# Score matmuls of two quadrants issued together, with the half convolution tap behind them

## The chip, the cores and the metric

The kernel runs on one core of a Trainium2 chip. The metric is device time in microseconds (us) of one execution; three runs are shown for the kernel before. Engines: TensorE (PE, with its weight loads shown apart as PEld), VectorE (DVE), ScalarE (ACT), GpSimd (POOL), and SyncE (SP), which issues the loads and stores.

## The reference

The input is x of shape (32, 32, 16, 16) in fp32: 32 images of 32 channels and 16 x 16 = 256 pixels. Two blocks follow one another. The first is a bias-free layer norm, a channel attention with a depthwise convolution beside it, and an MLP whose hidden layer (128 channels) goes through a depthwise 3 x 3 convolution. The second is a pixel attention. What the change touches is the hidden convolution and the pixel attention:

```python
# MLP of the first block
h = _gelu(_conv(x, fc1_w, fc1_b))
h = h + _gelu(_conv(h, pos_w, pos_b, groups=h.shape[1], pad=1))
return _conv(h, fc2_w, fc2_b)
# second block, per image; q, k, v are (b, 256 pixels, 32)
scores = jnp.einsum('bic,bjc->bij', q, k)
a = jax.nn.softmax(scores, axis=1)
x = jnp.einsum('bij,bjc->bic', a, v)
return X + x
```

## The kernel before

**Layout.** Channels lie on the partitions, and 128 partitions hold four images: quadrant q is partitions 32q to 32q + 31. Eight slots of four images make the batch of 32; a chunk k is two slots, 2k and 2k + 1. The hidden layer has 128 channels, so one image fills all partitions there (`hpad`, padded to 18 rows of 17). PSUM (`ps`) has eight banks of 512 fp32 columns; `LOW` is banks 0 to 3, `HIGH` banks 4 to 7.

**Engines.** The order on every engine is written out by hand, and semaphores join them. TensorE's program is the list of calls from L488 on. The chunks take turns in the order 1, 2, 0, 3. While the pixel attention of one chunk runs, TensorE computes the hidden convolution of the next one.

**The convolution on TensorE.** `conv_taps(k, lo, hi, banks, groups, rows)` (L366 to L377) does taps of chunk k with diagonal 32 x 32 weights. One tap is 16 matmuls: for each bank g of four, one for each row quadrant r of the array, so that each of the array's 16 tiles of 32 x 32 is used once. The position of a tap in `TAP_ORDER` sets how many columns a matmul has: 512 for the centre, 480 for a shift in one direction, 450 for a corner. With `rows` cut to two quadrants a call does half a tap, 8 matmuls on half of the tiles. The last tap raises `conv_done`.

**The pixel scores.** `scores` (L451) computes the scores of a quadrant with matmuls of 32 rows and 128 columns of weights. `scores_beside_tap` (L460) does two quadrants of a slot with tiles of 32 x 32 instead, which leaves the other two row quadrants of the array free: each half `jt` of 128 pixels takes 2 x 4 = 8 matmuls of 256 columns. Between the two halves it issues half a tap of the next chunk's convolution on the two quadrants that the scores leave free (L470, L471). The last score matmul raises `scores_done`. The inner loops over q and c are one matmul each (L467).

There are four such calls, each after a wait for `exp_done`, ScalarE's count of finished exponentials, which says that the score banks are free again:

```python
scores_beside_tap(3, (0, 1), LOW, 5, HIGH)     # L586, waits exp_done 2
conv_taps(2, 6, 7, HIGH)
scores_beside_tap(3, (2, 3), LOW, 5, HIGH)     # L589, waits exp_done 4
conv_taps(2, 7, 9, HIGH)
values(1, 0)                                   # L592, waits exp_done 5
...
scores_beside_tap(5, (2, 3), HIGH, 6, LOW)     # L609, waits exp_done 10
conv_taps(3, 7, 8, LOW)
scores_beside_tap(5, (0, 1), HIGH, 6, LOW)     # L612, waits exp_done 12
fc2_units(0, 6)                                # L614, waits exp_done 13
```

Position 5 of the taps has 480 columns, position 6 has 450.

**Who reads the scores.** VectorE's `maxima` (L961 to L965) waits for `scores_done` and reduces each bank to its negated row maxima. ScalarE's `pixel_exp` (L742 to L753) waits for `max_ready` and turns a bank into exponentials, two instructions for each quadrant, with the row sums beside them, and raises `exp_done`.

**Around the calls.** `values` on TensorE (L441, matmuls at L448) projects the values of a chunk; VectorE's `values` (L955, L957) adds the bias into `v_tok`. After it VectorE does five `conv_steps` (L917; it does chunk 0's convolution itself) and `finish_block_slot` (L927), which writes `X` of chunk 2. TensorE waits for that `X` before `queries_and_keys` (L420). `fc2_units` (L413) is a product with weights of 128 rows.

Of the kernel before, what the change touches and what calls it, by code (L numbers as in the profile page):

```python
# [63 lines left out]
def quadrant(q):  # L64
    return slice(C * q, C * (q + 1))

def rotated(g, t):
    return (g + t) % G

def build(nc, x_in, first_in, second_in, third_in, out):
    with ExitStack() as ctx:
# [45 lines left out]
        def c3(name):  # L119
            return third[:, THIRD_COLS[name][0]:THIRD_COLS[name][1]]  # L120

        def slot(buf, s):
            return buf[:, s // 2, (s % 2) * NPIX:(s % 2 + 1) * NPIX]
# [7 lines left out]
        def padded(buf, first, n, tap):  # L131
            dy, dx = TAPS[tap]
            off = first * IMAGE + INNER + dy * ROW + dx
            return buf[:, off:off + n * IMAGE].rearrange("p (i y s) -> p i y s", i=n, s=ROW)[:, :, 0:SIDE, 0:SIDE]

        def inside(images, tap):
            dy, dx = TAPS[tap]
            return images[:, :, max(0, -dy):SIDE - max(0, dy), max(0, -dx):SIDE - max(0, dx)]

        def pixels(ap):  # L140
            return ap.rearrange("p (i y s) -> p i y s", y=SIDE, s=SIDE)

        def h_first(k, g):
            return (G * k + g) * 2
# [111 lines left out]
        def _(pe):  # L256
# [109 lines left out]
            def conv_taps(k, lo, hi, banks, groups=range(G), rows=range(G)):  # L366

                for i in range(lo, hi):
                    tap = TAP_ORDER[i]
                    for g in groups:  # L370
                        for r in rows:
                            last = pe.matmul(inside(pixels(ps[quadrant(rotated(r, g)), banks[g], :]), tap),  # L372
                                             c3("taps")[quadrant(r), tap * C:(tap + 1) * C],
                                             inside(padded(hpad[quadrant(r), :], h_first(k, g), 2, tap), tap),
                                             start=i == 0, stop=i == 8)
                if hi == 9:
                    last.then_inc(conv_done, 1)  # L377
# [82 lines left out]
            def scores_beside_tap(s, quadrants, banks, tap, conv_banks):  # L460

                rows = [r for r in range(G) if r not in quadrants]
                for jt in range(2):
                    for q in quadrants:
                        for c in range(G):
                            at = jt * P + c * C
                            last = pe.matmul(ps[quadrant(c), banks[q], jt * NPIX:(jt + 1) * NPIX],  # L467
                                             slot(swapped, s)[quadrant(q), at:at + C],
                                             slot(rstd, s)[quadrant(q), :], start=True, stop=True)
                    if jt == 0:  # L470
                        conv_taps(s // 2 + 1, tap, tap + 1, conv_banks, rows=rows)  # L471
                last.then_inc(scores_done, 1)

            def weighted_values(s, bank):

                if s < SLOTS - 1:
                    pe.wait_ge(v_scaled, slot_turn(s) + 1)
                for jt in range(2):
                    if s == SLOTS - 1:
                        pe.wait_ge(last_v_scaled, jt + 1)  # L480
                    for g in range(G):
                        at = jt * P + g * C
                        last = pe.matmul(ps[quadrant(g), bank, 0:NPIX], v_tok[:, s, at:at + C],  # L483
                                         prob[:, G * (slot_turn(s) % PROBS) + g, jt * NPIX:(jt + 1) * NPIX],
                                         start=jt == 0, stop=jt == 1)
                last.then_inc(av_done, 1)
# [97 lines left out]
            conv_taps(2, 3, 5, HIGH)  # L584
            pe.wait_ge(exp_done, 2)
            scores_beside_tap(3, (0, 1), LOW, 5, HIGH)  # L586
            conv_taps(2, 6, 7, HIGH)
            pe.wait_ge(exp_done, 4)
            scores_beside_tap(3, (2, 3), LOW, 5, HIGH)  # L589
            conv_taps(2, 7, 9, HIGH)  # L590
            pe.wait_ge(exp_done, 5)
# [15 lines left out]
            conv_taps(3, 4, 6, LOW)  # L607
            pe.wait_ge(exp_done, 10)
            scores_beside_tap(5, (2, 3), HIGH, 6, LOW)  # L609
            conv_taps(3, 7, 8, LOW)  # L610
            pe.wait_ge(exp_done, 12)
# [557 lines left out]
```

## Time and profile before

| what | us |
|---|---|
| runs | 119.53, 121.95, 118.51 |
| median of the runs | 119.53 |
| the profiled execution, its own time | 119.45 |
| its span, first to last instruction | 117.7 |
| TensorE matmul busy | 101.3 |
| TensorE weight loads busy | 58.4 |
| ScalarE busy | 86.7 |
| VectorE busy | 75.2 |
| GpSimd busy | 12.1 |

Busy times are unions over the span, so two matmuls on different tiles at the same moment count once, and a matmul's time runs from its start to the landing of its last column. A row of the timeline merges instructions of one kind that start near each other: its start, the time from the first start to the last end, and their count. What stands in square brackets at a row's end is how long the engine had been idle before it and what ended that. The chain of work that ended last is followed back from the end: each piece is what the next one had waited for, or what stood before it on its engine.

### The profile page before, as it was taken

Reading aid. Unit: us, or ns where it says so; the run is one execution under the profiler, and the core shown is the slowest. Engines: PE = TensorE matmul, PEld = TensorE weight load, DVE = VectorE, ACT = ScalarE, POOL = GpSimd, SP = SyncE. Lnnn points to the kernel's source line nnn. Section 1 sums busy time; section 2 is a strip of 40 time slices with the busy share of each in tenths; the row PEclk is TensorE's granted clock in tenths of the full one; section 3 lists DMA queues with packets and bytes.
Section 4 is the critical chain, followed back from the end, with each engine's and each line's share of the span. In section 5 each row is a group of like instructions: output and inputs, shape, how many; then the busy total and the mean of one; then the engine's idle time right before and its main releaser. Section 6 shows DMA issues by size and latency. Waiting matters only on the chain.

```text
span 117.7 us, 5736 instructions
## 1 busy us (share of the span) xinstructions
PE 101.3 (86%) x2632; PEld 58.4 (50%) x2632; DVE 75.2 (64%) x152; ACT 86.7 (74%) x204; POOL 12.1 (10%) x22
## 2 busy tenths in 40 slices
PE   0394999789999899998999799999799999997660
PEld 0042677566684446832445464534364566575330
DVE  0007992133332989799957698964746579789851
ACT  4069991851785883889567989947889989898960
POOL 5010000000000000000000000598000040002300
PEclk9999999995589999999999999999999999999999
DMA  2880000000000000000000000000000020002022
GB/s 61 277 336 16 0 6 6 0 6 0 6 6 6 8 0 6 8 6 0 6 0 6 0 6 6 0 0 6 6 6 0 0 95 0 6 15 77 0 89 89
DMA packets 1751, 3.42 MB, mean 29 GB/s; under 512 B 320, under 2 KB 576, under 8 KB 1728
## 3 DMA queue, kind: packets, MB, share of 16 engines
q1 hardware_dynamic: 1584, 3.03, 7.4%
q8 instruction: 20, 0.33, 1.2%
q10 hardware_dynamic: 144, 0.03, 0.2%
q14 instruction: 3, 0.02, 0.1%
HBM read 2.01 MB, written 1.05 MB: 26 GB/s over the span
## 4 chain that ended last, share of the span: by engine, by line
PE 64%; ACT 16%; DVE 11%; DMA 3%; issue 3%; ACTq 0%; DVEq 0%
PE ps L372 13%; PE ps L295 10%; ACT prob L749 6%; PE ps L455 6%; PE ps L420 4%; PE ps L483 4%; ACT hpad L700 4%; DVE unit L917 3%; DMA first<-first_in 3%; PE ps L284 3%; PE ps L262 3%; PE ps L467 3%; PE ps L448 3%; ACT prob L736 3%; PE ps L307 2%
## 5 line engine op out<-in xcount | busy, mean ns | idle before, releaser
L372 PE MATMUL ps<-hpad,third 32*32 32x450 f32 (+2 forms) x864 | 36.5, 563 | 0.6 <-ACT hpad L700 0.5
L749 ACT ACTIVATE prob<-ps,smax 128x256 f32<-128x256 f32 x56 | 25.7, 479 | 3.7 <-DVE smax L964 3.7
L917 DVE SCALAR_TENSOR_TENSOR unit<-hpad,third,unit 128x544 f32<-128x544 f32 x32 | 23.8, 796 | 0.0
L964 DVE TENSOR_REDUCE smax<-ps 128x2 f32<-128x512 f32 x26 | 16.5, 683 | 6.5 <-PE ps L467 3.4
L372 PEld LDWEIGHTS ps<-hpad,third 32*32 32x32 f32 x864 | 14.0, 103 | 8.9 <-issue 4.2
L295 PE MATMUL ps<-npad,second 32*32 32x225 f32 (+2 forms) x576 | 14.6, 390 | 0.3 <-DVE npad L841 0.3
L239 POOL TENSOR_TENSOR v_tok<-v_tok,row_inv 128x256 f32<-128x256 f32 x7 | 5.1, 738 | 94.0 <-DVE row_inv L974 94.0
L700 ACT ACTIVATE hpad<-ps,third 128x1024 f32<-128x1024 f32 x8 | 8.7, 1116 | 4.5 <-PE ps L356 2.4
L749 ACT ACTIVATION_READ_ACCUMULATOR prob<-ps,smax 128x1 f32 x56 | 11.8, 211 | 0.0
L295 PEld LDWEIGHTS ps<-npad,second 32*32 32x32 f32 x576 | 9.2, 107 | 3.4 <-issue 1.7
L483 PE MATMUL ps<-prob,v_tok 128*32 128x256 f32 x128 | 8.1, 382 | 2.3 <-ACT prob L736 1.1
L669 ACT ACTIVATE swapped<-ps 128x512 f32<-128x512 f32 x8 | 4.4, 593 | 7.1 <-PE ps L262 7.1
L841 DVE SCALAR_TENSOR_TENSOR npad<-x,first,rstd 128x256 f32<-128x256 f32 x8 | 3.5, 479 | 9.5 <-ACT rstd L678 9.5
L455 PE MATMUL ps<-rstd,swapped 32*128 32x256 f32 x96 | 8.4, 397 | 0.5 <-ACT swapped L718 0.5
L262 PE MATMUL ps<-x,first 32*32 32x256 f32 x64 | 3.9, 566 | 4.9 <-DMA first<-first_in 4.9
L455 PEld LDWEIGHTS ps<-rstd,swapped 32*128 32x128 f32 x96 | 5.9, 184 | 3.7 <-DVE rstd L934 2.1
L273 PE MATMUL ps<-swapped,first 32*32 32x256 f32 x128 | 6.0, 508 | 1.7 <-ACT swapped L669 1.7
L709 ACT ACTIVATE acc<-ps,third 128x512 f32<-128x512 f32 x12 | 7.3, 688 | 0.0
L483 PEld LDWEIGHTS ps<-prob,v_tok 128*32 128x32 f32 x128 | 4.0, 109 | 6.2 <-issue 2.8
L467 PE MATMUL ps<-rstd,swapped 32*32 32x256 f32 x128 | 5.8, 384 | 1.2 <-ACT prob L749 1.2
L675 ACT ACTIVATE rstd<-ps,eps_col 128x512 f32<-128x512 f32 x8 | 5.4, 679 | 1.8 <-PE ps L273 1.8
L420 PE MATMUL ps<-X,third 32*32 32x256 f32 x128 | 6.4, 382 | 0.2 <-DVE X L927 0.2
(83 smaller groups left out, 140.4 us busy)
## 6 DMA issues: line engine op xcount, KB each, us to landing
x<-x_in SPq DMA_DIRECT2D x4, 256.0 KB, 5.2
y<-m SPq DMA_DIRECT2D x3, 256.0 KB, 2.5
third<-third_in SPq DMA_DIRECT2D x1, 456.5 KB, 6.5
second<-second_in SPq DMA_DIRECT2D x1, 453.5 KB, 5.4
y<-m SPq DMA_DIRECT2D x2, 128.0 KB, 1.9
first<-first_in ACTq DMA_DIRECT2D x1, 33.0 KB, 4.1
```

Of the source, the lines that this page charges most:

```text
L262: last = pe.matmul(ps[quadrant(rotated(g, s)), banks[s % 4], 0:NPIX], c1("centre")[quadrant(g), :], slot((x, res1)[ln], s)[quadrant(g), :] ...
L295: last = pe.matmul(inside(pixels(ps[quadrant(rotated(g, s)), banks[t], 0:NPIX]), tap), c2("attn_taps")[quadrant(g), tap * C:(tap + 1) * C] ...
L372: last = pe.matmul(inside(pixels(ps[quadrant(rotated(r, g)), banks[g], :]), tap), c3("taps")[quadrant(r), tap * C:(tap + 1) * C], inside(p ...
L420: last = pe.matmul(ps[quadrant(rotated(g, s)), bank, half * NPIX:(half + 1) * NPIX], c3(w)[quadrant(g), :], slot(X, s)[quadrant(g), :], st ...
L455: last = pe.matmul(ps[:, banks[q], jt * NPIX:(jt + 1) * NPIX], slot(swapped, s)[quadrant(q), jt * P:(jt + 1) * P], slot(rstd, s)[quadrant( ...
L467: last = pe.matmul(ps[quadrant(c), banks[q], jt * NPIX:(jt + 1) * NPIX], slot(swapped, s)[quadrant(q), at:at + C], slot(rstd, s)[quadrant( ...
L483: last = pe.matmul(ps[quadrant(g), bank, 0:NPIX], v_tok[:, s, at:at + C], prob[:, G * (slot_turn(s) % PROBS) + g, jt * NPIX:(jt + 1) * NPI ...
L700: act.activation(padded(hpad, h_first(k, g), 4, CENTRE), two(banks).rearrange("p g (t y s) -> p (g t) y s", t=2, s=SIDE), ACT.Gelu, bias=c ...
L709: act.activation(acc_buf(k, g), ps[:, banks[g], :], ACT.Gelu, bias=c3("pos_b")[:, g:g + 1]).then_inc(conv_gelu, 1)
L749: last = act.activation(prob[:, G * (slot_turn(s) % PROBS) + g, jt * NPIX:(jt + 1) * NPIX], ps[:, banks[q], jt * NPIX:(jt + 1) * NPIX], AC ...
L917: dve.scalar_tensor_tensor(out=sums, in0=source, scalar=weight, in1=sums, op0=ALU.mult, op1=ALU.add).then_inc(unit_step, 1)
L964: dve.tensor_reduce(smax[:, s, 2 * q:2 * q + 2], ps[:, banks[q], :].rearrange("p (j i) -> p j i", j=2), AX_X, ALU.max, negate=True).then_i ...
```

## The change

`scores_beside_tap` issues the matmuls of both halves one after the other, 16 in all, then raises `scores_done` on the last of them, and only then issues the half tap. The same matmuls are issued on the same operands and banks. The four calls and everything around them stay as they are.

```diff
--- before.py
+++ after.py
@@ -467,9 +467,8 @@
                             last = pe.matmul(ps[quadrant(c), banks[q], jt * NPIX:(jt + 1) * NPIX],
                                              slot(swapped, s)[quadrant(q), at:at + C],
                                              slot(rstd, s)[quadrant(q), :], start=True, stop=True)
-                    if jt == 0:
-                        conv_taps(s // 2 + 1, tap, tap + 1, conv_banks, rows=rows)
                 last.then_inc(scores_done, 1)
+                conv_taps(s // 2 + 1, tap, tap + 1, conv_banks, rows=rows)
 
             def weighted_values(s, bank):
 
```

TensorE's program at the first two calls (L586, L589), as a difference of the two orders; L467 is a score matmul, L372 a matmul of a tap, and the number at a row's end is how many stand together:

```order
 L372 MATMUL ps<-hpad,third 32x2x15x15 x16
 L372 MATMUL ps<-hpad,third 32x32x15 x16
-L467 MATMUL ps<-rstd,swapped 32x256 x8
+L467 MATMUL ps<-rstd,swapped 32x256 x16
 L372 MATMUL ps<-hpad,third 32x32x15 x8
-L467 MATMUL ps<-rstd,swapped 32x256 x8
 L372 MATMUL ps<-hpad,third 32x2x15x15 x16
-L467 MATMUL ps<-rstd,swapped 32x256 x8
+L467 MATMUL ps<-rstd,swapped 32x256 x16
 L372 MATMUL ps<-hpad,third 32x32x15 x8
-L467 MATMUL ps<-rstd,swapped 32x256 x8
 L372 MATMUL ps<-hpad,third 32x2x240 x16
```

The eight scores of the second half have moved ahead of the half tap (the `x8` of L372), which now stands directly ahead of the full tap (`x16`).

TensorE's program at the last two calls (L609, L612), with the product over 128 rows (L413) behind the second of them:

```order
 L372 MATMUL ps<-hpad,third 32x32x15 x32
-L467 MATMUL ps<-rstd,swapped 32x256 x8
+L467 MATMUL ps<-rstd,swapped 32x256 x16
 L372 MATMUL ps<-hpad,third 32x2x15x15 x8
-L467 MATMUL ps<-rstd,swapped 32x256 x8
 L372 MATMUL ps<-hpad,third 32x2x240 x16
-L467 MATMUL ps<-rstd,swapped 32x256 x8
+L467 MATMUL ps<-rstd,swapped 32x256 x16
 L372 MATMUL ps<-hpad,third 32x2x15x15 x8
-L467 MATMUL ps<-rstd,swapped 32x256 x8
 L413 MATMUL ps<-unit,third 32x512 x4
```

Here it is the same move; in the last call the half tap now stands between the scores and L413.

## Rows read from the trace of the kernel before

**Rows 1.** The page: TensorE's busy time among the engines', and the chain by engine.

```profile
PE 101.3 (86%) x2632; PEld 58.4 (50%) x2632; DVE 75.2 (64%) x152; ACT 86.7 (74%) x204; POOL 12.1 (10%) x22
...
PE 64%; ACT 16%; DVE 11%; DMA 3%; issue 3%; ACTq 0%; DVEq 0%
```

**Rows 2.** The chain in order of time, first pair: start us, us, what.

```profile
69.40 1.96 PE ps L372 x58
71.36 1.10 PE ps L448 x8
...
72.49 0.69 DVE v_tok L957
...
73.29 2.40 DVE unit L917 x3
...
77.51 0.80 DVE X L927 x2
...
78.36 0.45 PE ps L420 x8
```

**Rows 3.** The same chain, from the second pair on.

```profile
84.81 0.45 PE ps L467 x8
...
88.30 1.00 PE ps L413 x8
...
104.31 1.09 PE ps L455 x8
...
105.42 0.70 DVE smax L964
```

**Rows 4.** The timeline of VectorE, first pair: start us, us, instruction, [idle before].

```profile
67.34 1.29 DVE L964 TENSOR_REDUCE smax<-ps 128x2 f32<-128x512 f32 x2 [0.93 <-PE ps L467]
...
72.49 0.69 DVE L957 TENSOR_TENSOR v_tok<-ps,third 128x512 f32<-128x512 f32 x1 [0.37 <-PE ps L448]
```

**Rows 5.** The timeline of ScalarE at slot 3's first quadrant.

```profile
68.06 0.47 ACT L749 ACTIVATE prob<-ps,smax 128x256 f32<-128x256 f32 x1 [0.36 <-DVE smax L964]
...
68.89 0.20 ACT L749 ACTIVATION_READ_ACCUMULATOR prob<-ps,smax 128x1 f32 x1
```

**Rows 6.** The timeline of TensorE, first call, and its wait for X.

```profile
65.94 0.45 PE L467 MATMUL ps<-rstd,swapped 32*32 32x256 f32 x8 [0.62 <-ACT prob L749]
66.00 0.64 PE L372 MATMUL ps<-hpad,third 32*32 32x480 f32 x8
66.18 0.59 PE L467 MATMUL ps<-rstd,swapped 32*32 32x256 f32 x9
66.43 0.61 PE L372 MATMUL ps<-hpad,third 32*32 32x480 f32 x8
66.59 0.50 PE L467 MATMUL ps<-rstd,swapped 32*32 32x256 f32 x8
66.83 0.54 PE L372 MATMUL ps<-hpad,third 32*32 32x450 f32 x1
66.83 0.47 PE L467 MATMUL ps<-rstd,swapped 32*32 32x256 f32 x7
67.04 1.22 PE L372 MATMUL ps<-hpad,third 32*32 32x450 f32 x31
...
78.36 0.45 PE L420 MATMUL ps<-X,third 32*32 32x256 f32 x8 [0.24 <-DVE X L927]
```

**Rows 7.** Line L467: its matmul passes, ns min/median/max.

```profile
L467 PE MATMUL ps<-rstd,swapped x128: 372/375/399, 65.9 to 87.9; 32*32 32x256 f32 x128
```

**Rows 8.** The timeline of TensorE, third call.

```profile
84.81 0.45 PE L467 MATMUL ps<-rstd,swapped 32*32 32x256 f32 x8 [0.59 <-ACT prob L749]
84.87 0.61 PE L372 MATMUL ps<-hpad,third 32*32 32x450 f32 x8
85.05 0.59 PE L467 MATMUL ps<-rstd,swapped 32*32 32x256 f32 x9
85.27 0.59 PE L372 MATMUL ps<-hpad,third 32*32 32x450 f32 x8
85.46 0.50 PE L467 MATMUL ps<-rstd,swapped 32*32 32x256 f32 x8
```

## Prediction

> **What bounds the kernel now.** I began with the page. TensorE (PE) is the busiest engine, 101.3 of 117.7 us, and the chain of work that ended last runs 64% through it, against 16% for ScalarE (ACT) and 11% for VectorE (DVE) [rows 1]. The share alone doesn't say that PE sets the time at the four calls that change, so I read the chain in order of time next. Around the first two calls it goes along PE without a break from 65.94 to 71.36 us, through the scores (L467), the convolution taps (L372) and into the value projection (L448); there it passes to DVE, which turns the projected values into v_tok at 72.49, does five steps of its own convolution and writes X, and at 78.36 PE takes up again on that X [rows 2]. From 84.81 on it is PE again, through the third and fourth calls and on to a score product that ends at 105.40; then the tail of maxima, exponentials and the last products ends the program [rows 3].
>
> So both pairs of calls lie on the path. The engines beside PE confirm it. DVE stands idle for 0.93 us before the maxima of 67.34 and for 0.37 us before v_tok at 72.49, both times until a matmul ends [rows 4]; ACT waits 0.36 us at 68.06 for the maximum [rows 5]. The value product at 71.29 waits for the fifth set of exponentials (exp_done 5). Slot 2 gives four of these, and the first quadrant of slot 3 has its two exponentials from 68.06 on, with the last read-out over at 69.09 [rows 5]: more than two us early. PE reaches the value product when its own queue is through, and no earlier exponential would bring it forward.
>
> The telling place is the second half's eight scores. Their tiles are free from 66.42 on (66.18 + 0.24). One of them begins there: the group of 66.18 counts nine instead of eight and ends 0.59 later, so its ninth pass began at 66.18 + 0.59 - 0.37 = 66.40. The others don't: the next group begins at 66.59 [rows 6]. In program order the call's matmuls are 1 to 8 (scores), 9 to 16 (tap), 17 to 24 (scores). Number 17 runs, number 18 comes 0.04 us after number 1 has ended (66.18 + 0.37 = 66.55). The same again behind the taps: of the next full tap one record starts at 66.83, the next ones at 67.04, when tap matmul number 9 has ended at 66.43 + 0.56 = 66.99. The reading that fits both: PE looks across about 17 matmuls from the oldest unfinished one, starts any whose tile is free, and takes in another only when the oldest has ended. The third call repeats it: 84.81, 84.87, 85.05, 85.27, and then 85.46 where the tiles were free at 85.29 [rows 8].
>
> The Trainium skill ("TensorE: Matmul & The Clock Gate", spec table and the step-by-step section of part 2) gives TensorE a queue of 64 with a partial reorder window that pulls weight loads ahead, while matmuls stay in program order. The depth agrees with this trace (16 matmuls with two loads and two passes each are 64 records). The strict order doesn't: the first scores' second passes start at 66.18, after passes of the tap that stands behind them. By strict order nothing would overlap in either version and the edit would be worth nothing.
>
> **The change, part by part.** Nothing is added or removed: in each of four calls the same 8 + 8 + 8 matmuls are issued as 8 + 8 + 8 with the tap last. No DMA, bank, semaphore or wait on another engine changes; `scores_done` hangs on the last score as before. The order pieces show what moves: 16 score matmuls stand together and the tap joins the full tap behind it.
>
> What it takes: the tap becomes numbers 17 to 24. Number 17 can start at once, 18 to 24 only when number 1 ends, at 66.59, in place of 66.00. Until then two row quadrants of the array stand still. What it gives: the second half's scores are in the window from the start, and go at 66.40 to 66.45 (eight starts 7 ns apart, as the first half's) instead of 66.59 to 66.69. Their last second pass begins 0.22 later, at 66.66 or so, and ends at 67.03 instead of 67.30, where the group of 66.83 ends [rows 6], so `scores_done` comes 0.27 us earlier in a call that starts from an idle PE (first and third). I cost that gain at nothing: what it feeds is DVE's 0.93 us idle and ACT's exponentials, and PE waits for neither, as shown above. It costs nothing the other way either.
>
> The price on PE: number 18 enters at 66.59 in both versions, and the matmul that can enter when 18 ends is ready accordingly. Before, 18 is a score and ends 0.61 later, at 67.20; after, it is a tap matmul and ends 0.99 later, at 67.58. The 35th matmul, and behind it the last six of the following tap, go 0.38 us later. I stepped both orders through with these four rules (tile free, 17 open, end in order, 17 ns between entries once the queue is full). For the order of before this gives 71.37 for the end of the last tap behind the second call and 88.30 for the last score of the fourth, where the chain has 71.36 and 88.30 [rows 2, 3]. For the changed order it gives:
> - first and second call, tap of 480 columns: 0.38 us each, 0.75 in all after rounding;
> - third call, tap of 450 columns: 0.40 to the second pass (84.87 to 85.27) and 0.54 for that pass, 0.94 against 0.61: 0.33 us [rows 8];
> - fourth call, the same tap, but behind it comes a product over 128 rows (L413), which starts when everything has drained [rows 3]. Before, the last to drain is a score at 88.30; after, it is the tap's last matmul, 0.27 us behind what the third call already moved.
>
> Sum: 0.75 + 0.33 + 0.27 = 1.35 us. The bounds of a call's price: nothing, if the quadrants really work apart; and the tap wholly exposed, 8 tap matmuls alone at 0.99 + 0.05 = 1.04 us less the 0.27 that the scores come earlier, 0.77. I take the stepped value because it reproduces two ends of before.
>
> Does it arrive at the end? The first 0.75 moves L448, then v_tok, which DVE awaits with 0.37 us of idle [rows 4]; DVE then has no gap up to X, and PE awaits X at 78.36 [rows 2]. If PE had slack there, the 0.75 would vanish; PE idles 0.24 us there until DVE has X [rows 6], so the late side is DVE's and nothing is absorbed. The other 0.60 stands at 88.30, and PE runs on from there to 105.40 without waiting [rows 3]. So 119.45 (the profiled execution's own time: 117.7 span and what lies around it) + 1.35 = 120.80 us. The median of the runs shown is 119.53, 0.08 above the profiled one, too little to correct for.
>
> **Rivals.**
> 1. *The quadrants hide it.* Per tile the work is unchanged: rows of the scores 4 x 0.22 to 0.24 = 0.9 us, rows of the tap 2 x 0.43 = 0.86. If the tap may start whenever its tiles are free, the call takes 0.9 in either order and the time stays at 119.5. For it: the tap does start 0.06 us after the scores in the present order. Against it: the score of 66.59 with its tile free at 66.42. The Trainium skill ("TensorEngine Tiling (Array Packing)", key properties) says that different tiles execute in parallel and independently; by that alone the sum is zero, and the pause at 66.42 speaks against taking it alone.
> 2. *Faster.* The maxima come earlier: 0.27 us in the first and third call. If the exponentials set when PE may go on, this comes through, 119.45 - 0.54 = 118.9 us. It decides from the point where PE waits for exp_done behind a call. For it: PE did wait for ACT 0.62 us at 65.94 [rows 6] and 0.59 at 84.81 [rows 8]. Against it: those waits are ahead of the calls, not behind them.
> 3. *The tap stands bare.* The window opens for the tap only as the last score ends, so each call costs 0.77: 4 x 0.77 = 3.1, 122.5 us. Place: behind the sixteenth score. Against it: number 18 starts in the trace while 9 to 17 are under way.
> 4. *Only the first pair counts.* Between 88.3 and 105.4 ACT and DVE wait too, and the chain may change hands there: 119.45 + 0.75 = 120.2 us.
>
> **How the numbers follow.** The forecast has 0.68, rival 1 0.12, rival 2 0.07, rival 3 0.07, rival 4 0.06. The likeliest is 120.8 us. The range goes from 119.4 (rival 1, below it only rival 2) to 122.0 (a price per call of 0.64, between stepped and bare). About 2%, 2.4 us, is what a measurement of this kernel can tell from no change. Slower by more needs 121.9 or above: rival 3 and a sliver of the forecast, 0.08. Faster by more needs under 117.1, which no case gives: 0.01. Within 2%: 0.91.
>
> **What would show it.** In the profile after: one group of 16 score passes from 65.94 with the second half's first pass at about 66.40; the tap's first passes at about 66.59 but for one; maxima at 67.07 in place of 67.34; L448 at about 72.0 in place of 71.29; v_tok 0.75 later; L413 some 1.35 later than 88.23. If L448 stands at 71.3 and the tap starts near 66.2, rival 1 holds. If DVE's or ACT's chain carries the earlier maxima to the end, rival 2. If the tap starts at 67.0, rival 3. The forecast is wrong altogether if PE's stretch from scores to L448 is as long as before.

## The result, and the profile after

The changed kernel's first four runs have a median of 121.25 us (120.72 to 124.97), the kernel before 119.07 (118.51 to 121.95, four runs). The ratio is 1.0222 with a 95% interval of 1.0157 to 1.0286. Measured again with twelve runs, it has a median of 121.09 us against 119.84 (35 runs of the kernel before). Both ratios compare only the undisturbed executions, since some executions of either kernel take some per cent longer than the rest; in the second comparison the ratio is 0.9995 (0.9930 to 1.0061). The two intervals don't meet, and neither holds the 1.011 that 1.35 us would be: the times scatter by more than the effect and settle neither its size nor, by themselves, its sign, so both have to be read in the traces.

The page and the chain of the changed kernel; below the busy time per engine, the chain in order of time: start us, us, what.

```profile
PE 101.2 (85%) x2632; PEld 57.0 (48%) x2632; DVE 75.5 (63%) x152; ACT 86.9 (73%) x204; POOL 12.1 (10%) x22
...
PE 64%; ACT 15%; DVE 11%; issue 4%; DMA 4%; ACTq 0%; DVEq 0%
```

```profile
73.17 0.69 DVE v_tok L956
...
79.04 0.45 PE ps L420 x8
...
89.58 1.00 PE ps L413 x8
...
106.70 0.70 DVE smax L963
```

TensorE's busy time over the whole span, 101.2 us against 101.3 [rows 1], doesn't show the loss, because ahead of the calls something else differs: the kernel before ran there for 6.8 us at the lower of the two clock levels (1.2 of 2.4 GHz, granted clock 0.50 from the 27th to the 33rd us) and was busy for 56.08 us up to the first call, the changed kernel had no such stretch and 54.68. From the first call to the maxima at 105.42 and 106.70 it is busy for 38.42 us before and 39.77 after, 1.35 more: the same passes side by side less often. The chain takes the same way [rows 2, 3], and each step is late. The first call starts at 65.87, 0.07 us earlier than before; X is taken up at 79.04 instead of 78.36, L413 stands in the chain at 89.58 instead of 88.30, the maximum behind the last chained score product at 106.70 instead of 105.42: 1.28 us later, and with the 0.07 of the start 1.35.

The timeline of TensorE in the changed kernel, first call, then the two products that follow the pairs, and the third call's start.

```profile
65.87 0.67 PE L467 MATMUL ps<-rstd,swapped 32*32 32x256 f32 x16 [0.63 <-ACT prob L748]
66.30 0.56 PE L372 MATMUL ps<-hpad,third 32*32 32x480 f32 x1
66.33 0.42 PE L467 MATMUL ps<-rstd,swapped 32*32 32x256 f32 x8
66.52 0.60 PE L372 MATMUL ps<-hpad,third 32*32 32x480 f32 x2
...
66.59 0.37 PE L467 MATMUL ps<-rstd,swapped 32*32 32x256 f32 x1
66.61 1.69 PE L372 MATMUL ps<-hpad,third 32*32 32x480 f32 x36
...
71.97 1.16 PE L448 MATMUL ps<-third,X 128*128 128x128 f32 x8
...
85.49 0.67 PE L467 MATMUL ps<-rstd,swapped 32*32 32x256 f32 x16 [0.60 <-ACT prob L748]
...
89.51 1.07 PE L413 MATMUL ps<-unit,third 128*32 128x512 f32 x8
```

Compare with [rows 6]. The sixteen passes of the first half run through (65.87), the second half's first passes follow at 66.33, without the pause before. The tap, which had begun 0.06 us behind the scores, now has one matmul at 66.30 and the rest from 66.52 on: 0.65 us behind the call's start, just when the first score has ended. From the first call to L448 it is 71.97 - 65.87 = 6.10 us (before 71.29 - 65.94 = 5.35), from the third call to L413 89.51 - 85.49 = 4.02 (before 88.23 - 84.81 = 3.42). Sum of the two losses: 0.75 + 0.60 = 1.35 us.

VectorE in the changed kernel, in order of time:

```profile
67.07 1.29 DVE L963 TENSOR_REDUCE smax<-ps 128x2 f32<-128x512 f32 x2 [0.73 <-PE ps L467]
...
73.17 0.69 DVE L956 TENSOR_TENSOR v_tok<-ps,third 128x512 f32<-128x512 f32 x1 [0.95 <-PE ps L448]
```

The maxima of the first call did come earlier (67.07 against 67.34 in [rows 4], 0.20 after taking off the earlier start), and it is worth nothing: before v_tok VectorE now waits 0.95 us for L448 where it waited 0.37.

### The profile page after: what moved, and what is told of

Its sections match the earlier page's. It is cut to its first block, busy times and chain, and to the rows that moved or that the text cites. A ratio compares the mean times of both kernels' runs of the same rounds, so it can differ in the third digit from the quotient of the medians.

```text
span 118.9 us, 5736 instructions
## 1 busy us (share of the span) xinstructions
PE 101.2 (85%) x2632; PEld 57.0 (48%) x2632; DVE 75.5 (63%) x152; ACT 86.9 (73%) x204; POOL 12.1 (10%) x22
## 2 busy tenths in 40 slices
DMA packets 1751, 3.42 MB, mean 29 GB/s; under 512 B 320, under 2 KB 576, under 8 KB 1728
## 4 chain that ended last, share of the span: by engine, by line
PE 64%; ACT 15%; DVE 11%; issue 4%; DMA 4%; ACTq 0%; DVEq 0%
PE ps L372 13%; PE ps L295 11%; ACT prob L748 6%; PE ps L455 6%; PE ps L420 4%; PE ps L482 4%; DMA first<-first_in 4%; DVE unit L916 3%; PE ps L284 3%; PE ps L356 3%; PE ps L448 3%; ACT prob L735 3%; PE ps L262 3%; PE ps L467 2%; PE ps L273 2%
## 5 line engine op out<-in xcount | busy, mean ns | idle before, releaser
L372 PE MATMUL ps<-hpad,third 32*32 32x450 f32 (+2 forms) x864 | 37.2, 563 | 0.6 <-issue 0.4
L372 PEld LDWEIGHTS ps<-hpad,third 32*32 32x32 f32 x864 | 14.5, 103 | 10.5 <-issue 5.6
L295 PE MATMUL ps<-npad,second 32*32 32x240 f32 (+2 forms) x576 | 14.3, 367 | 1.6 <-issue 1.3
L295 PEld LDWEIGHTS ps<-npad,second 32*32 32x32 f32 x576 | 7.9, 103 | 5.6 <-issue 4.1
L273 PE MATMUL ps<-swapped,first 32*32 32x256 f32 x128 | 5.3, 446 | 1.5 <-ACT swapped L668 1.4
L467 PE MATMUL ps<-rstd,swapped 32*32 32x256 f32 x128 | 5.3, 378 | 1.2 <-ACT prob L748 1.2
```

The costliest lines, as they stand in the source:

```text
L273: last = pe.matmul(ps[quadrant(g), banks[s % 4], 0:NPIX], c1("mean")[quadrant(q), :], slot(swapped, s)[quadrant(q), :], start=True, stop=True)
L295: last = pe.matmul(inside(pixels(ps[quadrant(rotated(g, s)), banks[t], 0:NPIX]), tap), c2("attn_taps")[quadrant(g), tap * C:(tap + 1) * C] ...
```

## The experiments

In all of them two distances are read in the profile: from the first call's start to L448, and from the third call's start to L413. Before they are 5.35 and 3.42 us, changed 6.10 and 4.02.

**The changed kernel again** (no edit).

> The changed kernel once more, unaltered, to settle its size. Theory (17 matmuls open in order, price on TensorE's path): +1.35 us in the profile between the start of the first call and the product L413, and about 1.1 to 1.2% in the time. The first ratio, 1.022, would be 1.2 us more than that path shows; if it comes again, half of the loss lies outside the two pairs of calls or in something the profile of one execution does not carry. Rival (tiles work apart): ratio 1.00.

```profile
65.74 0.66 PE L467 MATMUL ps<-rstd,swapped 32*32 32x256 f32 x16 [0.64 <-ACT prob L748]
...
71.84 1.16 PE L448 MATMUL ps<-third,X 128*128 128x128 f32 x8
...
85.36 0.67 PE L467 MATMUL ps<-rstd,swapped 32*32 32x256 f32 x16 [0.59 <-ACT prob L748]
...
89.38 1.07 PE L413 MATMUL ps<-unit,third 128*32 128x512 f32 x8
```

6.10 and 4.02 us again, to the hundredth. The times are those of the second comparison above: the first ratio's 2.2% doesn't come again, and the 1.1 to 1.2% that was expected isn't shown by it either. Of the scatter there is more at the end.

**One pair at a time.** Two kernels, against the kernel before. The first has the new order in the first pair of calls; in the second kernel 3 and 5 stand the other way round:

```diff
-                    if jt == 0:
+                    if jt == 0 and s == 5:
                         conv_taps(s // 2 + 1, tap, tap + 1, conv_banks, rows=rows)
                 last.then_inc(scores_done, 1)
+                if s == 3:
+                    conv_taps(s // 2 + 1, tap, tap + 1, conv_banks, rows=rows)
```

> Only the first two calls (slot 3) have the new order; the last two keep the old one. Theory: the value product L448 0.75 us later against the first call's start, nothing behind it, so +0.75 us in the time. If the loss is not additive (a wait further on swallows it): 0.

```profile
65.17 0.67 PE L467 MATMUL ps<-rstd,swapped 32*32 32x256 f32 x16 [0.63 <-ACT prob L751]
...
71.28 1.16 PE L448 MATMUL ps<-third,X 128*128 128x128 f32 x8
...
84.79 0.45 PE L467 MATMUL ps<-rstd,swapped 32*32 32x256 f32 x8 [0.58 <-ACT prob L751]
...
88.21 1.07 PE L413 MATMUL ps<-unit,third 128*32 128x512 f32 x8
```

6.11 and 3.42: the loss sits in the first pair alone.

> Only the last two calls (slot 5) have the new order. Theory: L413 0.60 us later against the third call's start, +0.60 us in the time. Rival (only the first pair counts, slack of ScalarE and VectorE behind 88 us): 0. With the first-pair kernel's the two must add up to the changed kernel's loss.

```profile
64.70 0.45 PE L467 MATMUL ps<-rstd,swapped 32*32 32x256 f32 x8 [0.63 <-ACT prob L751]
...
70.05 1.16 PE L448 MATMUL ps<-third,X 128*128 128x128 f32 x8
...
83.57 0.66 PE L467 MATMUL ps<-rstd,swapped 32*32 32x256 f32 x16 [0.59 <-ACT prob L751]
...
87.59 1.07 PE L413 MATMUL ps<-unit,third 128*32 128x512 f32 x8
```

5.35 and 4.02. The two losses add up, and nothing between or behind them changes: from L448 to the third call it is 13.51 us in the one (84.79 - 71.28) and 13.52 in the other (83.57 - 70.05), as before (84.81 - 71.29 = 13.52). From L413 to the maxima behind the last chained score product it is 17.19 us in both, as before (105.42 - 88.23) and in the changed kernel (106.70 - 89.51), so no slack swallows the second loss either, which rules out the fourth rival. The medians, 120.17 and 120.09 us against 119.84, are too coarse for it (ratios 1.0068, 0.9995 to 1.0141, and 1.0000, 0.9937 to 1.0064).

**The tap first.** The half tap ahead of both score halves:

```diff
+                conv_taps(s // 2 + 1, tap, tap + 1, conv_banks, rows=rows)
                 for jt in range(2):
                     for q in quadrants:
...
-                    if jt == 0:
-                        conv_taps(s // 2 + 1, tap, tap + 1, conv_banks, rows=rows)
```

> In all four calls the half tap is issued ahead of both score halves. Its eight matmuls start with the scores at once, so row quadrants do not stand still at the call's start. Theory of the 17 open matmuls: number 18 is then a score, but it enters only when the first tap matmul has ended (0.99 us instead of 0.61), so the loss is as large as in the changed kernel: L448 +0.73, L413 +0.65 more, +1.4 us in all; and scores_done comes later, 67.7 where before it was 67.3. Rival (what costs is that two quadrants idle while the tap waits behind 16 scores): no loss on TensorE against before.

```profile
64.43 0.64 PE L372 MATMUL ps<-hpad,third 32*32 32x480 f32 x8 [0.63 <-ACT prob L748]
64.49 0.66 PE L468 MATMUL ps<-rstd,swapped 32*32 32x256 f32 x16
64.86 0.61 PE L372 MATMUL ps<-hpad,third 32*32 32x480 f32 x8
65.04 0.91 PE L468 MATMUL ps<-rstd,swapped 32*32 32x256 f32 x9
...
65.69 0.47 PE L468 MATMUL ps<-rstd,swapped 32*32 32x256 f32 x7
...
70.52 1.16 PE L448 MATMUL ps<-third,X 128*128 128x128 f32 x8
...
84.03 0.61 PE L372 MATMUL ps<-hpad,third 32*32 32x450 f32 x8 [0.59 <-ACT prob L748]
...
88.10 1.07 PE L413 MATMUL ps<-unit,third 128*32 128x512 f32 x8
```

Here tap and scores start together (64.43 and 64.49) and all four row quadrants are at work from the first moment, and still the pair costs 6.09 us, the second 4.07 (expected 6.08 and 4.07). The scores end at 66.16, 1.73 us behind the start, where it was 1.36 before. So it isn't the idle quadrants at the call's start that cost. It is that the ends are taken in order: a matmul that stays open long at the head of the queue holds back everything behind it. The tiles-work-apart rival falls with this. The time is 120.73 us (ratio 1.0044, 0.9967 to 1.0122).

**Half as many columns in the half tap**, in the order of the changed kernel and in that of before. Both leave out the half taps' second image.

```diff
-            def conv_taps(k, lo, hi, banks, groups=range(G), rows=range(G)):
+            def conv_taps(k, lo, hi, banks, groups=range(G), rows=range(G), images=2):
...
-                            last = pe.matmul(inside(pixels(ps[quadrant(rotated(r, g)), banks[g], :]), tap),
+                            last = pe.matmul(inside(pixels(ps[quadrant(rotated(r, g)), banks[g], 0:images * NPIX]), tap),
...
-                conv_taps(s // 2 + 1, tap, tap + 1, conv_banks, rows=rows)
+                conv_taps(s // 2 + 1, tap, tap + 1, conv_banks, rows=rows, images=1)
```

> The order of the changed kernel, with each matmul of the four half taps cut to one of its two images: 240 or 225 columns instead of 480 or 450 (the half tap of the second image is left out). Theory: the price is the length of the tap matmul that stands as number 18; now it is as short as a score, so nothing is lost against before. From the first call's start to L448 5.3 us (before 5.35, changed 6.10), from the third call's start to L413 3.3 to 3.4 us (before 3.42, changed 4.02). If the loss came from the tap's late start as such, half of it would stay: 5.7 and 3.7.

```profile
68.28 0.67 PE L467 MATMUL ps<-rstd,swapped 32*32 32x256 f32 x16 [0.64 <-ACT prob L748]
...
73.59 1.16 PE L448 MATMUL ps<-third,X 128*128 128x128 f32 x8
...
87.10 0.67 PE L467 MATMUL ps<-rstd,swapped 32*32 32x256 f32 x16 [0.59 <-ACT prob L748]
...
90.41 1.07 PE L413 MATMUL ps<-unit,third 128*32 128x512 f32 x8
```

> The order of before with the same narrow half taps (the half tap of the second image left out). Theory: number 18 is a score in any case and enters when score number 1 ends, so half of the tap's columns less changes nothing at all: 5.35 and 3.42 us. If TensorE were bound by the columns that its tiles stream, it would gain some 0.2 us per call.

```profile
67.63 0.45 PE L467 MATMUL ps<-rstd,swapped 32*32 32x256 f32 x8 [0.63 <-ACT prob L749]
...
72.98 1.16 PE L448 MATMUL ps<-third,X 128*128 128x128 f32 x8
...
86.49 0.45 PE L467 MATMUL ps<-rstd,swapped 32*32 32x256 f32 x8 [0.59 <-ACT prob L749]
...
89.92 1.07 PE L413 MATMUL ps<-unit,third 128*32 128x512 f32 x8
```

With short tap matmuls the changed order takes 5.31 and 3.31 us: the whole loss of 1.35 is gone and 0.15 more. In the order of before the same cut of the tap brings nothing, 5.35 and 3.43. Fewer columns are worth 0.79 us in the first pair of one order and zero in the other. That is the plainest sign that in the order of before the stretch isn't bound by what the tiles stream. What counts is how long the matmul lasts that the next entry waits for.

**The tap behind twelve scores**:

```diff
                 for jt in range(2):
                     for q in quadrants:
+                        if jt == 1 and q == quadrants[1]:
+                            conv_taps(s // 2 + 1, tap, tap + 1, conv_banks, rows=rows)
...
-                    if jt == 0:
-                        conv_taps(s // 2 + 1, tap, tap + 1, conv_banks, rows=rows)
```

> The half tap behind twelve scores, between eight (before) and sixteen (changed). Theory, stepped by the same four rules: first pair as bad as the changed kernel, 5.35 + 0.74 = 6.09 us, since numbers 18 to 20 are taps again; second pair 3.42 + 0.27 = 3.69, since the last matmuls before the drain are scores. scores_done of the first call stays at 1.37 us behind its start. If the price grew evenly with the tap's place, it would be half: 5.72 and 3.72.

```profile
65.65 0.45 PE L469 MATMUL ps<-rstd,swapped 32*32 32x256 f32 x8 [0.64 <-ACT prob L749]
...
71.76 1.16 PE L448 MATMUL ps<-third,X 128*128 128x128 f32 x8
...
85.27 0.45 PE L469 MATMUL ps<-rstd,swapped 32*32 32x256 f32 x8 [0.59 <-ACT prob L749]
...
89.00 1.07 PE L413 MATMUL ps<-unit,third 128*32 128x512 f32 x8
```

6.11 and 3.73 us (expected 6.09 and 3.69). Moving the tap half as far costs the full price in the first pair, since number 18 is a tap matmul again, and only half of it in the second, where scores are the last to drain.

**No tap beside the scores.** The pairs of half taps become whole ones:

```diff
             scores_beside_tap(3, (0, 1), LOW, 5, HIGH)
-            conv_taps(2, 6, 7, HIGH)
+            conv_taps(2, 5, 6, HIGH)
             pe.wait_ge(exp_done, 4)
             scores_beside_tap(3, (2, 3), LOW, 5, HIGH)
-            conv_taps(2, 7, 9, HIGH)
+            conv_taps(2, 6, 9, HIGH)
```

(`scores_beside_tap` issues only its sixteen scores; the second pair likewise.)

> No tap beside the scores: sixteen scores alone on two row quadrants, and the two half taps of each pair joined into one whole tap behind the first call. Theory: L448 5.35 + 0.60 = 5.95 us behind the first call's start, L413 3.42 + 0.51 = 3.93 behind the third's: the two idle quadrants cost less than the changed kernel's half taps behind the scores (6.10 and 4.02). If overlap of tiles were what counts, this would be the slowest of all: 8 scores x 2 halves bare, at least 0.4 us per call worse than the changed kernel.

```profile
65.07 0.88 PE L467 MATMUL ps<-rstd,swapped 32*32 32x256 f32 x24 [0.64 <-ACT prob L748]
...
71.03 1.16 PE L448 MATMUL ps<-third,X 128*128 128x128 f32 x8
...
84.54 0.67 PE L467 MATMUL ps<-rstd,swapped 32*32 32x256 f32 x16 [0.59 <-ACT prob L748]
...
88.47 1.07 PE L413 MATMUL ps<-unit,third 128*32 128x512 f32 x8
```

5.96 and 3.93 us, as expected (5.95 and 3.93), and less than the changed kernel's 6.10 and 4.02. Placed behind sixteen scores, the half tap is worse than no pairing of scores and tap at all.

The times of the last four kernels don't follow these distances. Against 118.56 us of the kernel before (seven runs) their medians of four runs are 121.20 (narrow, changed order; ratio 1.0212, 1.0125 to 1.0298), 120.47 (narrow, order of before), 120.41 (twelve scores; 1.0175, 1.0116 to 1.0233) and 121.86 (no tap beside). The first of them is shorter than the kernel before in both distances and still slower in its time, and the second, equal in both, has a higher median too. What makes the difference lies outside the two pairs, and in the profiles only the stretch ahead of the first call is left for it; the last section has what the traces show of that.

## Why the prediction was right

The range of 119.4 to 122.0 holds the 121.25 us, and the forecast of 120.8 is 0.45 below. Like with like, profiled execution against profiled execution, it is 120.72 us after 119.45: 1.27 more, where 1.35 was forecast. That the total comes so close is in part luck, because the stretch ahead of the calls scatters by over 3 us and happened to bring both kernels to the first call at nearly the same moment (65.94 and 65.87). The distances behind it are no luck. Point by point:

- *PE's path carries both pairs.* Right: L448, v_tok, X, the third call and L413 all moved by what the pair ahead had lost.
- *About 17 matmuls are open, taken out in order of their ends.* Right in all that it was used for: eight kernels with distances worked out beforehand came within 0.04 us. One detail was off. Number 17, the first tap matmul, was to start at once, which in the changed kernel is about 65.98 (sixteen entries 7 ns apart behind 65.87); it starts at 66.30. The rows show what it waits for. A first pass of a score lasts up to 0.40 us [rows 7], so number 1's first pass ends at 65.87 + 0.40 = 66.27, and number 17 starts 0.03 later. In the tap-first kernel number 1 is a tap matmul, whose first pass ends at about 65.02 (the group of 64.43, 0.64 long, less 0.05 for its eight starts). Number 17, a score whose tile is free at 64.95 (64.49 + 0.24 + 0.22), starts at 65.04. This reads as if passes were counted: 32 are open, the first pass of 17 enters when the first pass of 1 has ended, and 18 follows when the second has. It costs nothing here, since 18 and not 17 decides. No kernel was made to test the two counts against each other.
- *0.75 us for the first pair, 0.33 + 0.27 for the second.* Measured 0.75 and 0.60. How the 0.60 divides between the third and fourth call wasn't read apart.
- *The earlier maxima are worth nothing.* Right. The last score pass of the first call ends 1.09 us behind the call's start (66.59 + 0.37 - 65.87) where it was 1.36, the 0.27 of the forecast; the maxima begin only 0.20 earlier, 0.11 us behind that end instead of 0.04. Why is not known.
- *1.35 us, of 119.45.* The path of the profiled execution lost 1.35. The run times can't confirm it: the two comparisons give 1.022 and 0.9995. The "slower by over 2%" that had 0.08 would have been the verdict on the first one by its middle, and the repeat doesn't bear it out.

Of the rivals, the first (quadrants hide it) fell with the changed kernel's own distances and the tap-first kernel. The second (faster through the maxima) fell with the idle time before v_tok, and because between 62 and 90 us TensorE waits for ScalarE's exponentials only ahead of the first and third call, 0.6 us each, before and after alike. The third (tap bare, 0.77 a call) fell with the measured 0.75 for two calls and with the tap's start at 66.52, not 67.0, and the fourth with the second pair alone. A rival that the prediction doesn't name is that the second half waits for the first half's results, since both write to the same banks. The changed kernel excludes it: there the second half starts at 66.33, while the first half's passes run on to 66.54 (65.87 + 0.67).

One sentence of the prediction goes too far, that by strict order nothing would overlap. Eight scores start 7 ns apart on eight tiles in strict order and do overlap. What strict order excludes is a later matmul's pass ahead of an earlier matmul's, as at 66.00 and 66.18 [rows 6]; what such an order would have cost was not worked out.

## What to carry to other kernels

When small matmuls on different tiles are to run side by side, it isn't enough that their tiles are free: TensorE here kept some sixteen to seventeen fp32 matmuls (32 passes) open and took in the next only when the oldest had ended. Put short matmuls where others wait for their end, keep long ones away from that place, and look in the timeline for a group that starts later than its tile comes free. A change of 1% in a kernel whose runs scatter by over 5% (117.64 to 124.27 us in 35 runs) is read as distances between fixed points of the trace, not in the run times.

## What was not expected of the hardware

The runs scatter far ahead of the calls. From the first matmul to the first call it is 61.07 us in the profile of before (4.87 to 65.94), and 59.4 to 62.9 us in the ten profiles of this study, though the instructions of that stretch are the same; from L448 to the third call it is 13.51 to 13.52 us in all ten, and from L413 to the maxima behind the last chained score product 17.19 to 17.22. The longest of them is the narrow tap in the changed order. One stretch of it, and below it the same stretch in the changed kernel; L284 is a product of tokens on the whole array:

```profile
14.33 3.67 PE L284 MATMUL ps<-second,parity 128*128 128x64 f32 x16
17.94 2.95 PE L295 MATMUL ps<-npad,second 32*32 32x225 f32 x96
20.82 1.10 PE L307 MATMUL ps<-qk_tok,second 128*128 128x64 f32 x8
```

```profile
13.42 2.00 PE L284 MATMUL ps<-second,parity 128*128 128x64 f32 x16
15.35 1.99 PE L295 MATMUL ps<-npad,second 32*32 32x225 f32 x96
17.27 1.10 PE L307 MATMUL ps<-qk_tok,second 128*128 128x64 f32 x8
```

The same 16 passes take 3.67 us and 2.00, the same 96 take 2.95 and 1.99, and from 20.8 us on the two agree. The clock probably explains this one, though the page's clock row doesn't show it: the first entry that the trace has of a granted clock, full speed, stands at 20.5 us in this profile and at 8.8 to 10.7 us in the other nine, and the page counts the time without an entry as full speed. That TensorE was still at the lower level until 20.5 us is inferred from this and from the slow passes. It doesn't explain the rest of the scatter: the changed kernel's first profile has no stretch at the lower level behind its first entry and needs 60.78 us up to the first call (65.87 - 5.09), its second has one of 6.8 us around the 30th us, as before has, and needs 60.78 as well. What makes the difference there was not tried.
